# The expert choice taken from the first half of a feed-forward step, ScalarE evicting both halves, and the weights fetched right behind the choice

## The reference

```
def step(h, p):
    op = jnp.argmax(h[0, 0, :NOPS])
    q, k, v = h @ p['wq'][op], h @ p['wk'][op], h @ p['wv'][op]
    attn = softmax(einsum('bqd,bkd->bqk', q, k) * scale)
    y = einsum('bqk,bkd->bqd', attn, v) @ p['wo'][op]
    h = where(p['am'][op], y, h)
    z = relu(h @ p['w1'][op] + p['b1'][op]) @ p['w2'][op] + p['b2'][op]
    h = where(p['fm'][op], z, h)
```

## Time and profile before

| | us |
|---|---|
| median of 3 runs | 405.33 |
| the profiled execution, its own time | 405.59 |
| its span in the profile | 403.8 |
| TensorE matmul busy | 352.2 (87%) |
| VectorE busy | 232.8 (58%) |
| ScalarE busy | 166.6 (41%) |
| GpSimd busy | 14.6 (4%) |

### The profile page before, as it was taken

The page is one execution under the profiler, slowest core; times in us unless marked ns, Lnnn a source line. Parts: engine busy times, 40 slices in busy tenths (PEclk is TensorE's granted clock), DMA queues, the critical chain, the costliest instruction groups (busy, mean ns, idle before and its releaser), DMA issues.

```text
span 403.8 us, 11255 instructions
## 1 busy us (share of the span) xinstructions
PE 352.2 (87%) x4989; PEld 199.3 (49%) x4989; DVE 232.8 (58%) x287; ACT 166.6 (41%) x158; POOL 14.6 (4%) x30
## 2 busy tenths in 40 slices
PE   6798399999999997698558999477799999999996
PEld 4534035763333333554113344343586667777774
DVE  1593968999999995554994884336411121112112
ACT  1374558787899952131005765312211111111110
POOL 3034000000000002000000000000000000000000
PEclk9989779999999999989999999979999999999999
DMA  5119400000000007200000000000000000000001
GB/s 152 22 29 348 147 0 2 2 2 2 2 2 2 2 2 261 72 2 15 2 0 2 0 2 2 2 0 0 2 2 3 2 5 3 3 3 3 3 3 41
DMA packets 9767, 11.57 MB, mean 29 GB/s; under 512 B 3894, under 2 KB 8888, under 8 KB 9720
## 3 DMA queue, kind: packets, MB, share of 16 engines
q1 hardware_dynamic: 9352, 9.55, 7.2%
q0 software_dynamic: 224, 1.10, 0.8%
q10 hardware_dynamic: 144, 0.20, 0.2%
HBM read 10.44 MB, written 0.40 MB: 27 GB/s over the span
## 4 chain that ended last, share of the span: by engine, by line
PE 62%; DVE 24%; issue 6%; DMA 3%; ACT 2%; SPq 2%; DVEq 1%; ACTq 0%
PE PS L867 62%; DVE pool_ L713 9%; DVE TOPS L767 4%; DMA PAR<-in_par 1%; DVE RSC L499 1%; DVE TMP L685 1%; DMA W1R<-in_fwa 1%; DMA W4R<-in_aw 1%; SPq L217 1%; DVE pool_ L537 0%; DVE ASEG L635 0%; DVE MSC L630 0%; DVE TMP L497 0%; DVEq L768 0%; ACT pool_ L418 0%
## 5 line engine op out<-in xcount | busy, mean ns | idle before, releaser
L867 PE MATMUL PS<-pool_,CON 128*32 128x392 f32 (+2 forms) x1320 | 113.4, 503 | 1.1 <-DVE pool_ L713 0.6
L377 ACT ACTIVATE pool_<-TMP,WA 128x3136 f32<-128x3136 f32 x27 | 78.4, 2931 | 18.9 <-PE PS L867 15.4
L713 DVE TENSOR_SCALAR pool_<-TMP,WA 128x3136 f32<-128x3136 f32 x45 | 81.8, 1851 | 5.6 <-PE PS L867 5.5
L867 PEld LDWEIGHTS PS<-pool_,CON 128*32 128x32 f32 (+1 forms) x1320 | 49.7, 112 | 63.1 <-issue 47.7
L856 DVE COPY pool_<-PS 128x392 f32<-128x392 f32 x32 | 18.1, 567 | 84.0 <-PE PS L867 84.0
L465 ACT ACTIVATE pool_<-PS 128x392 f32<-128x392 f32 x32 | 15.9, 498 | 85.8 <-PE PS L867 85.8
L867 PE MATMUL PS<-pool_,WS 128*32 128x136 f32 (+3 forms) x1024 | 46.4, 333 | 0.0
L867 PE MATMUL PS<-HE,WS 128*32 128x136 f32 (+3 forms) x1024 | 46.3, 333 | 0.0
L867 PEld LDWEIGHTS PS<-pool_,WS 128*32 128x32 f32 x1024 | 33.0, 110 | 13.8 <-issue 8.1
L867 PEld LDWEIGHTS PS<-HE,WS 128*32 128x32 f32 x1024 | 32.6, 111 | 14.4 <-issue 8.4
L867 PE MATMUL PS<-CON 128*128 128x196 f32 (+1 forms) x142 | 29.0, 349 | 1.9 <-DMA W4R<-in_aw 1.0
(11 more groups left out here) (203 smaller groups left out, 292.1 us busy)
## 6 DMA issues: line engine op xcount, KB each, us to landing
pool_<-in_pho SPq DMA_DIRECT2D x1, 3144.0 KB, 10.7
HE<-in_phe SPq DMA_DIRECT2D x1, 3136.0 KB, 14.2
CW<-in_cw SPq DMA_DIRECT2D x2, 576.0 KB, 4.5
CON<-in_con POOLq DMA_DIRECT2D x1, 732.5 KB, 6.0
out_y<-Y SPq DMA_DIRECT2D x1, 392.0 KB, 2.4
CON<-in_con POOLq DMA_DIRECT2D x1, 337.0 KB, 4.8
CQ<-in_ws SPq DMA_DIRECT2D x16, 9.0 KB
MPP<-in_mpp SPq DMA_DIRECT2D x1, 256.0 KB, 2.6
```

The lines of the kernel that those rows point to most:

```text
L377: a.activation(RING[:, g % RG, :, :].rearrange("p b (r c) -> p b r c", r=SIDE), window(n // CQ), ACT.Abs, bias=WA2[:, n:n + 1], scale=-1.0 ...
L713: v.tensor_scalar(RING[:, g % RG, :, :].rearrange("p b (r c) -> p b r c", r=SIDE), window(n // CQ), WA2[:, n:n + 1], None, ALU.max).then_i ...
L867: return t.matmul(out_, lhsT, rhs, start=start, stop=stop, skip_group_check=True)
```

## The change

`B2C` is a new one-column tile, into which VectorE copies the bias `b2` at the start of a feed-forward. ScalarE evicts both halves with it. The semaphore `ffn_h` starts at 1 (a memset on GpSimd), so that the unchanged wait of TensorE for `k * 2 + 2` now passes after the first half. VectorE waits for both halves before the residual sum, and TensorE waits for the residual sum (`x2_ready`) at the start of the next attention and of the next feed-forward. The first choice waits for three writes of `ln_out` in place of four. SyncE's issues become a function `fetch()` that is called in front of the loop, and in the loop directly behind the wait for the next choice.

```
+        B2C = sb("B2C", [P, 1])
...
 block.sync
+            def fetch():
+                sp.load(raw, KINT[0:1, 0:1], bass_reorder=False)
+                sp.reg_mov(code, sp.snap(raw) & (OPW - 1))
+                c = sp.snap(code, min_val=0, max_val=4 * NB + 7)
                 op = NOPS - (sp.snap(raw, ...) >> OPW.bit_length() - 1)
                 sp.reg_mov(which, (NB - (c >> 2)) * NOPS + op)
                 w = sp.snap(which, min_val=0, max_val=NB * NOPS - 1)
...
+            sp.wait_ge(s["decided"], 1)
+            fetch()
+            sp.reg_mov(chosen, 1)
+            with active_steps(sp, code):
                 n = sp.snap(chosen, min_val=1, max_val=NB)
                 sp.wait_ge(s["decided"], n + 1)
                 sp.sem_inc(s["sp_woke"], 1)
                 sp.reg_add(chosen, chosen, 1)
-                sp.load(raw, KINT[0:1, 0:1], bass_reorder=False)
-                sp.reg_mov(code, sp.snap(raw) & (OPW - 1))
+                fetch()
 block.gpsimd
             g.memset(MB[:, :, :], 0.0).then_inc(s["zeroed"], 1)
+            g.memset(B2C[:, :], 0.0).then_inc(s["ffn_h"], 1)
 block.scalar
-                    a.wait_ge(s["ffn_out"], k * 2 + 1)
-                    a.activation(half(H, 0), bank(0), ACT.Identity, bias=B2S).then_inc(s["ffn_h"], 1)
+                    a.wait_ge(s["bias_kept"], k + 1)
+                    for h in range(2):
+                        a.wait_ge(s["ffn_out"], k * 2 + (h + 1))
+                        a.activation(half(H, h), bank(h), ACT.Identity, bias=B2C[:, :]).then_inc(s["ffn_h"], 1)
 block.vector
             decide(1)
+            v.wait_ge(s["ffn_h"], 1)
             residual()
...
+                    v.tensor_copy(B2C[:, :], B2S).then_inc(s["bias_kept"], 1)
                     for u in range(1, 8, 2):
                         v.wait_ge(s["ffn_h1"], k * 8 + (u + 1))
                         v.tensor_scalar(HIDT[:, u, :], bank(u), B1S, 0.0, ALU.add, ALU.max).then_inc(s["hid_dve"], 1)
-                    v.wait_ge(s["ffn_out"], k * 2 + 2)
-                    v.tensor_scalar(half(H, 1), bank(1), B2S, None, ALU.add).then_inc(s["ffn_h"], 1)
...
                 decide(n + 1)
+                v.wait_ge(s["ffn_h"], v.snap(nf, min_val=0, max_val=NB) * 2 + 1)
                 residual()
 block.tensor
-            t.wait_ge(s["ln_out"], 4)
+            t.wait_ge(s["ln_out"], 3)
...
                 with t.If((c & 1) > 0):
-                    k = t.snap(na, min_val=0, max_val=NB)
+                    k, n = t.snap(na, ...), t.snap(chosen, min_val=1, max_val=NB)
                     t.wait_ge(s["zeroed"], 4)
                     t.wait_ge(s["att_w"], k * 16 + 16)
+                    t.wait_ge(s["x2_ready"], n)
...
                 with t.If((c & 2) > 0):
-                    k = t.snap(nf, min_val=0, max_val=NB)
+                    k, n = t.snap(nf, ...), t.snap(chosen, min_val=1, max_val=NB)
                     t.wait_ge(s["ffn_wa"], k * 16 + 16)
+                    t.wait_ge(s["x2_ready"], n)
```

More of the change, by code:

```diff
@@ L203, in build @@
             "key_chain key_ready row_done decided "
-            "ffn_wa ffn_wb att_w ffn_h1 hid_act hid_dve ffn_out ffn_h att_proj keys_done q_done v_proj v_done "
+            "ffn_wa ffn_wb att_w ffn_h1 hid_act hid_dve ffn_out ffn_h bias_kept att_proj keys_done q_done v_proj v_done "
             "sc_done st_done top_step top_split top_rows row_act row_dve exp_done acc_done den_done pv_done num_out den_out att_scaled att_wo att_h "
@@ L244, in _ @@
             sp.dma_start(HO[:, :, :], bass.AP(pho.tensor, 0, [[1, P], [LO, NK], [1, NPH + 1]])).then_inc(s["strip_in"], 16)
-            sp.wait_ge(s["decided"], 1)
             code = sp.alloc_register("sp_code"); which = sp.alloc_register("sp_which")
             raw = sp.alloc_register("sp_raw")
-            sp.load(raw, KINT[0:1, 0:1], bass_reorder=False)
-            sp.reg_mov(code, sp.snap(raw) & (OPW - 1))
             chosen = sp.alloc_register("sp_chosen")
-            sp.reg_mov(chosen, 1)
-            with active_steps(sp, code) as c:
+            def fetch():
+                sp.load(raw, KINT[0:1, 0:1], bass_reorder=False)
+                sp.reg_mov(code, sp.snap(raw) & (OPW - 1))
+                c = sp.snap(code, min_val=0, max_val=4 * NB + 7)
                 op = NOPS - (sp.snap(raw, min_val=0, max_val=(NOPS + 1) * OPW - 1) >> OPW.bit_length() - 1)
@@ L979, in _ @@
                 with t.If((c & 1) > 0):
-                    k = t.snap(na, min_val=0, max_val=NB)
+                    k, n = t.snap(na, min_val=0, max_val=NB), t.snap(chosen, min_val=1, max_val=NB)
                     t.wait_ge(s["zeroed"], 4)
                     t.wait_ge(s["att_w"], k * 16 + 16)
+                    t.wait_ge(s["x2_ready"], n)
                     bridge()
@@ L1077, in _ @@
                 with t.If((c & 2) > 0):
-                    k = t.snap(nf, min_val=0, max_val=NB)
+                    k, n = t.snap(nf, min_val=0, max_val=NB), t.snap(chosen, min_val=1, max_val=NB)
                     t.wait_ge(s["ffn_wa"], k * 16 + 16)
+                    t.wait_ge(s["x2_ready"], n)
                     for h in range(2):
```

## The result

The changed kernel takes 399.5 us (median of 6 runs, 398.21 to 401.09) against 405.03 (6 runs) for the kernel before beside it: a ratio of 0.9867, 95% interval 0.9832 to 0.9903. The forecast was 403.5, its range 402.5 to 404.8: the sign was right, the gain is about three times the one forecast. Over all 26 executions of the changed kernel the median is 399.8, and over 96 of the kernel before 404.7, so some 4.9 us is the gain to explain.

A forecast was written before the change was run, and what follows sets the result against it. TensorE and VectorE alternate as bound; step one waits for TensorE's branch, step two for W4R's transfer. 0.26 - 0.20 + 0.76 + 0.50 - 0.07 - 0.20 + 0.79 = 1.84 off 405.59 gives 403.75, median 403.5; range 402.5 to 404.8.

The forecast's parts named there:

- item 2: First step, fetch in front of the loop: W1R comes earlier but TensorE is in its 4.776 us branch; worth 0.
- if the branch L979 changed its 4.8 us: Sign against the prediction: TensorE's branch over the attention section, taken in the first step, has another length.
- B: Rival: the longer loop body makes the jump behind the second choice a second far branch, 4.776 us; 407.0 us, chance 0.06.
- no gain and no loss: First feed-forward: TensorE's stillness stays as long, so the granted clock adds nothing, up to half a microsecond either way.
- Items 5 and 9: End of steps 1 and 2: the row starts behind half 0 and half 1's products; gains 0.76 and 0.79 us.
- Item 1: First choice: the row follows the first half, but VectorE's own second write holds the reduction; gain 0.26 us.
- Item 3: Feed-forward start, steps 1 and 2: TensorE's added wait costs 0.2 us each, bounds 0 and 0.3.
- Item 7: Second step: SyncE's loop back edge and tests no longer precede the W4R transfer; gain 0.50 us.
- Item 8: Attention: TensorE's satisfied wait for the residual sum remains behind the weights' landing; cost 0.07 us (0 to 0.1).
- Items 4 and 6: Feed-forward: B2C's copy (0.06 to 0.2 us) and half 1's eviction on ScalarE (0.59 for 0.62) are hidden.
- A: Rival: the new waits are free and the gap before W4R's DMA shrinks; gain 2.31 us, time 403.0, chance 0.29.
- C: Rival: in the second step W4R, issued earlier, does not land earlier; gain 1.34 us, time 404.0, chance 0.16.

The follow-up runs named there:

- p2_choice: Kernel before plus only the choice behind half 0, ScalarE's two evictions and the waits, SyncE in its old order: 401.72 us, ratio 0.9927.
- b_pad216: Kernel before plus 216 do-nothing semaphore increments on TensorE in the last 54 groups of the adder convolution: 402.24 us, ratio 0.9942.
- p2_again: p2_choice's program traced once more, nothing changed: 400.8 us (one run).
- p4_waits: Kernel before plus only TensorE's two added waits for x2_ready, in attention and feed-forward: 405.26 us, ratio 1.0025.
- p1_fetch: Kernel before plus only SyncE's fetch() in front of the loop and directly behind the wait for the choice: 403.64 us, ratio 0.9979.
- x_pad216: Changed kernel plus 216 do-nothing increments on TensorE in the last 54 groups of the adder convolution: 399.41 us, ratio 0.9889 to the kernel before.
- v_warm: Changed kernel with TensorE's warm-ups moved from each step's head to before the loop and each step's end: 402.12 us, ratio 0.9918 to the kernel before.
- v_both: v_warm plus the 216 do-nothing increments on TensorE: 399.1 us, ratio 0.9864 to the kernel before (ratio without one run of 404.57).
- v_near: Changed kernel with a copy of TensorE's feed-forward before the attention, so the first step takes no far branch: 401.2 us, ratio 0.9926 to kernel before.
- x_pad60: Changed kernel plus 60 do-nothing increments on TensorE in the adder convolution's last 30 groups: 403.06 us, ratio 0.9974 to the kernel before.

## Why the prediction was wrong, point by point

**The step that failed is item 2**, and the sentence in it that TensorE "is in its 4.776 us branch", taken as a constant that merely starts 0.26 earlier. It is 3.635 in the profile after and 3.53 to 3.72 in five more traces of that kernel or near it, 1.05 to 1.25 less. I had named "if the branch L979 changed its 4.8 us" as what would make the prediction wrong, but gave it no rival: I weighed only that a second such branch might appear (B), never that this one could shrink. What the runs showed in its place is a length with two values, by whether one or two instruction fetches lie in the branch. The rule that I cited for B bore on this side too. The Trainium skill ("Runtime: NRT & Kernel Launch", Instruction fetch mechanics) says that blocks of 16 KiB are fetched ahead in sequence, and that a taken branch out of them waits for its own fetch; the earlier trace rows gave the branch one number (the trace agrees with the blocks: 41 fetches on q8, 0.67 MB, 16 KB each), and the view of the DMA queues in that stretch would have shown two fetches within it, where one is enough. Alone the fetch takes 1.17 us (after); side by side they took 1.8 and 1.68 (before), 1.40 and 2.24 (p2_choice).

**The clock, said to bring "no gain and no loss"**, was the second failure and follows from the first. The prediction argued that the stillness stays as long as it was, which holds only for a constant branch. TensorE stood still for 1.48 us in front of the products in place of 2.52, the clock stayed at 1.00, and F1-R2 fell by 1.55, 0.55 more than the 1.00 that the row behind half 0 brings where the clock is the same in both (F2-R3). Over all twenty traces the granted clock of the first feed-forward's products is 0.50 to 0.62 in the seven where TensorE had stood still for 2.5 us or more, and 1.00 (once 0.96) in the thirteen with 2.04 or less. That the clock followed from the shorter stillness is read from this; no run changed the stillness alone.

These two are 1.14 + 0.55 = 1.7 us of the 2.74 missed between H0 and N. That they are not the change's logic is shown by the kernel before with b_pad216, which has the same 1.9 us from H0 to N without the change, and by p2_choice and p2_again, 2.2 us apart with the same program.

**Items 5 and 9, the row behind half 0: right mechanism, 0.76 and 0.79 forecast, 1.00 each measured at full clock** (F2-R3 5.31 and 4.31; for step 1 F1-R2 5.31 in b_pad216 and 4.31 after). The step that was mis-sized is "TensorE is in order and still runs half 1's products until ...". It took the modelled end of a group of products for the time at which the row can start, and in step 2 put the row 0.02 behind it. In the profile after the products are drawn until 248.79 + 0.86 = 249.65, and the row's matmul starts at 249.45, 0.20 before that. Its weights load at 249.28, 0.09 behind the end of ScalarE's half 0 (248.60 + 0.59 = 249.19), as they did behind VectorE's half 1 before; but the matmul follows its load by 0.17 in place of 0.03, so the products ahead do hold it a little. That is why 1.00 came and not the 1.16 by which the two evictions end apart in step 2. (In step 1 they end only 0.75 apart, on the lower clock; the prediction's 1.16 in item 5 is step 2's.)

**Item 1, the first choice: 0.26 forecast, 0.40 measured.** I had VectorE's reduction start 0.04 behind the end of its second half:

```profile
160.55 0.22 PE L877 MATMUL PS<-CON,H 128*1 128x32 f32 x2
...
161.07 0.16 DVE L745 TENSOR_REDUCE KMAX<-PS 1x1 f32<-1x19 f32 x1
```

The row is there by 160.77, and the reduction starts 0.30 later, 0.09 before the drawn end of the write (161.16). In the kernel before it started 0.04 behind the row. So VectorE's own write did set the start, as forecast, but not for the full length of its line in the timeline.

**Item 3, the added wait at a feed-forward's start: right, a little too dear.** From the branch's end to the first product it is 168.49 - 164.28 - 3.635 = 0.58, before 171.72 - 166.55 - 4.776 = 0.39, so 0.19 for the forecast 0.2; in step 2 A-F2 is 0.12 longer, again for 0.2. p4_waits has the same two, 0.14 to 0.19 and 0.10.

**Item 7, SyncE's second step: 0.50 forecast, 0.73 measured** (R2 to the issue of `W4R` 3.37 before, 2.64 after and in p1_fetch). The back edge and tests went as said: from the masked code's first register operation to the address computation it is 0.60 less. The rest, 0.12, lies in the gaps of the operations from there to the issue, the same number of them in both. `W4R` still ends last in front of the attention, as forecast. R2-A gains only 0.63, since the transfer took 3.11 in place of 3.02. Item 8's wait costs next to nothing: the attention's first product starts 0.05 behind the landing, before 0.03, for a forecast of 0.07.

**Items 4 and 6: right.** `B2C`'s copy takes 0.15 at 168.16 with VectorE idle behind it; half 1's eviction on ScalarE ends at 173.35, before the residual sum at 173.91.

**The rivals.** A had the right direction for SyncE (0.73) and for item 8, and was wrong on the waits of item 3. B didn't happen in any trace of the changed kernel. C is refuted: `W4R` landed 3.11 after its issue (before 3.02).

The sum by measured terms without branch and clock is, in the order of time, 0.40 + 0.06 (from R1 to the branch's start) - 0.19 + 1.00 + 0.63 - 0.12 + 1.00 + 0.12 = 2.90, and with 1.14 + 0.55 it is 4.59, against 4.58 in the traces. Where both kernels have the short branch (b_pad216 and x_pad216) H0 to N is 99.52 and 96.03, 3.5 us for the change alone, one trace each. Medians say less: b_pad216 and x_pad216 were timed on two chips, and their ratios, 0.9942 and 0.9889, are 0.5% or some 2.1 us apart.

**What stays open.** The long branch was seen in all four traces of kernels with the first choice and loop placed as before (4.73 to 5.07), in two of three of p2_choice's kind and in v_warm (4.37); the short one in all six of the changed kernel and its near kin. p2_choice and p2_again show that chance decides within a program; why the changed kernel falls on the short side so regularly was not found. The branch of v_warm says that it isn't a property of the change as such. The length of TensorE's stillness alone doesn't settle the clock everywhere either: it held behind 2.04 us in v_both and fell behind 1.71 in v_near. Where the neighbouring block's fetch is asked for isn't seen, only when its transfer begins. And 0.7 of the 1.8 us before H0 was not traced.

## What to carry to other kernels

A long branch in a trace isn't one number but a fetch or two, and its length can change with anything that moves code or time: count the instruction fetches inside it, give "it gets shorter" a chance of its own, and read the clock's consequence behind it. The drawn end of a group of instructions need not be when its engine takes the next: here the row's matmul started 0.20 us before it, and VectorE's reduction 0.09. Look in another place of the trace how close the next instruction came. And before a gain of one per cent is put down to a change, pad the program before it by instructions that do nothing: here that alone brought 0.6%, and with another number of them nothing (1.0008).

## What the runs showed of the hardware that was not expected

- A far taken branch on TensorE took 3.3 to 3.8 us with one instruction fetch in it (13 traces) and 4.4 to 5.1 with two (7 traces); the same branch not taken took 0.07.
- Around these branches an instruction fetch took 0.88 to 1.46 us alone. Where two ran side by side each took 1.16 to 2.44; in v_warm, where the second began as the first ended, 0.96 and 1.70.
- The 41 instruction fetches on q8 moved 0.67 MB, 16 KB each. 60 instructions that do nothing, put in front, were enough to break the first feed-forward's products in two (7.87 us in place of 4.31 in x_pad60).
- The exit shows the same with the clock: behind 4.23 us of stillness it is at 0.54, and with the 8 warm-up products moved there it is 1.00 behind 2.1 to 2.3 us, and the rest of the kernel 0.85 (v_both) to 1.35 us (v_warm) shorter, while the exit grows by 0.51 to 0.81.
